# Two blocks of layer-norm work moved out of the attended tiles and in between incidence products

## The chip, the cores and the metric

The kernel runs on one core of a Trainium2 chip. The metric is the device time of one execution in microseconds (us). The engines are PE (matrix products and transposes), DVE (vector), ACT (activations and copies out of PSUM), POOL (small elementwise work) and SP (which only issues DMAs here).

## What is computed

Four graph layers follow each other on 2048 nodes with 128 features, each on `relu(layernorm(x))`, each added to `x`. Cut to what matters here:

```
# layer 1: two steps of sparse attention, then a layer norm with gain and bias
for n in range(2):
    A  = top_p_attention(Xa)          # softmax rows cut to the largest that hold 0.9, renormed
    Xf = R @ Xf
    Xa = A @ Xa
    Z  = Z + Xf @ U1[n].T + Xa @ U2[n].T
h = X + Z
x = x + (h - mean(h)) / sqrt(var(h) + 1e-5) * ln_g + ln_b
# layer 2: incidence products
h = relu(layernorm(x))
m = adj.T @ h                         # "incidence products" below: 16 row tiles of adj
...
x = x + 0.5 * c + 0.5 * c @ W.T       # c from adj @ (m / sqrt(edge_degree)), degrees and h
```

Two layer norms stand between the attention and the incidence products: the first closes layer 1, the second opens layer 2.

## The kernel before, in words

The 2048 nodes are 16 tiles of 128 rows, in 4 blocks of 4 tiles. The attention works through 8 groups, 4 blocks in each of 2 steps; DVE cuts the rows of one group (a bound by guesses, then the rows above it) while PE multiplies the attended rows of the group before it. Each engine has its own instruction list, written by hand; order on an engine is the order of the code, and engines wait for each other by counting semaphores only.

**An attended tile** (`attend`, PE L481 transposes and L740 products, ACT L1001 copies) turns 16 pieces of 128 columns, ACT copies them out four at a time, PE multiplies them. Between its first two groups of four, PE also turns and projects the result of the tile before (L481, L705 to L707), which ACT writes to `R` with its row sum (L1185), counting `z_ok`.

**The last period** is group 7 on DVE (block 3 of step 1) while PE attends block 2's four tiles. As soon as step 1's results of a block stand in `R`, the block can be normed "ahead". For block b that is, in order:

- `first_norm` on ACT: the mean and four squares with sums (L1210, L1213), then on POOL `nd` (L448), the power `es` (L450) and the product `ri` (L452), in the order that `LN_ORDER` lists the blocks' two norms;
- `first_scaled` on ACT (L1228), four tiles, counting `ln_y`;
- `rows_turned` on PE, four transposes in two halves (L481), `turned_out` on ACT (L1001 into `ST`);
- `rows_summed` on PE, two halves, each twice three products (L785 to L787): gain, old `x` and bias;
- `summed_out` on ACT (L1243 into `K`), counting `ln_x2`, `second_norm` on ACT and POOL, `second_scaled` on ACT (L1257 into `hr`), counting `h2_act`.

`blocks_ahead(k)`, on PE and on ACT, says what of this follows the attended tile k. Before, block 0 and block 1 are interleaved there in halves; what is left of block 1 follows the fourth tile. Then PE runs `multiplied(t)`, an incidence product of tile t: four 128x512 products (L798) into PSUM banks 0 to 3. Four tiles of it come before block 2's norm, six after. Then PE attends the four tiles of block 3, turns, and finishes the products 10 to 15.

`multiplied(t)` waits for its adjacency tile, a 1 MB load from HBM which SP issues when the product four before has freed its buffer, and for `h2_act` of its block, 4 per block:

```
pe.wait_ge(here, count)
if t < RING:
    pe.wait_ge(h2_act, G * (t // G + 1))
```

On DVE, `under` of tile k in group 7 (L1419) waits for the last transposes of the attended tile k on PE, since it writes over what they read; `masked` (four L1419 at the group's end) follows the search for the cut.

Of the kernel before, what the change touches and what calls it, by code (L numbers as in the profile page):

```python
# [16 lines left out]
NT = N // P  # L17
DA = 64
BK = 512
G = BK // P  # L20
# [74 lines left out]
def gnn_kernel(nc, x, adj, W0, b0, W1, W2, W3, U1, U2, ln_g, ln_b, L2W, L3W, b3, out):  # L95
# [18 lines left out]
    with ExitStack() as ctx:  # L114
# [101 lines left out]
        def bank(b):  # L216
            return PS[:, b, :]
# [49 lines left out]
        LN_ROOTS = 3 * NB + 5  # L267
        AHEAD_BLOCKS = NB - 1
        RING = G * AHEAD_BLOCKS
        LN_ORDER = ((0, 0), (1, 0), (0, 1), (1, 1), (2, 0), (2, 1))  # L270
        ORDER = (1, 2, 3, 0)

        def natural(t):
# [4 lines left out]
            return (nat_in[t % G], 16 * (NB + 1 + t // G)) if t < RING else (nat_eb[t % G], 16)  # L278

        def turned_at(b, h):  # L280
            return bank(h if b < 2 else 4 + h)

        def summed_at(b, h):
            return bank(2 + h if b < 2 else 6 + h)

        def normed_at(b, second):

# [189 lines left out]
        def _(pe):  # L477
# [8 lines left out]
            with pe.Fori(0, NB) as i:  # L486
                for s in range(G):
                    t = i * G + s
# [274 lines left out]
            def rows_turned(b, h):  # L763

                pe.wait_ge(ln_y, G * (b + 1))
                if b == 1:
                    pe.wait_ge(ln_ts, h + 1)
                for k in range(2):
                    tr = turn(turned_at(b, h)[:, k * P:(k + 1) * P], R[:, G * b + 2 * h + k, :])
                tr.then_inc(ln_t, 1)  # L770

            def rows_summed(b, h):

                pe.wait_ge(ln_ts, 2 * b + h + 1)
                if b == 0:
                    pe.wait_ge(late_in, 16)
                    pe.wait_ge(bc_dma, 3 * 16)
                    pe.wait_ge(diag_ok, 1)
                elif b == 1:
                    pe.wait_ge(ln_x2, 2 * (h + 1))  # L780
                else:
                    pe.wait_ge(z_ok, NT + RING)
                for k in range(2):
                    to = summed_at(b, h)[:, k * P:(k + 1) * P]
                    pe.matmul(to, ST[0][:, (2 * h + k) * P:(2 * h + k + 1) * P], WT[:, U1T, :], start=True, stop=False)  # L785
                    pe.matmul(to, ident[:, :], K[:, G * b + 2 * h + k, :], start=False, stop=False)
                    mm = pe.matmul(to, ident[:, :], BC[:, LNB, :], start=False, stop=True)  # L787
                mm.then_inc(ln_x, 1)

            def multiplied(t):  # L790
                here, count = natural_in(t)
# [3 lines that stand above are left out]
                else:  # L795
                    pe.wait_ge(h2_ok, 1)
                for n in range(4):
                    mm = pe.matmul(bank(n), hr[:, t, :], natural(t)[:, n * BK:(n + 1) * BK],  # L798
                                   start=(t == 0), stop=(t == NT - 1))
                mm.then_inc(m_mm, 1)  # L800

            def blocks_ahead(k):

                if k > 0:
                    rows_summed((k - 1) // 2, (k - 1) % 2)
                rows_turned(k // 2, k % 2)

            def later_keys(n):

# [4 lines left out]
            for step in range(STEPS):  # L814
# [61 lines left out]
                if step == 0:  # L876
# [5 lines left out]
                    for k in range(G):  # L882
                        attend(0, NB - 1, k)

            rows_summed(1, 1)
            pe.wait_ge(ln_x2, 2 * G)
            for t in range(G):
                multiplied(t)
            for h in range(2):
                rows_turned(2, h)  # L890
                rows_summed(2, h)
            for t in range(G, 2 * G + 2):
                multiplied(t)
            for k in range(G):
                attend(1, NB - 1, k)
# [58 lines left out]
            for i in range(NB):  # L954
                b = ORDER[i]
# [38 lines left out]
        def _(act):  # L994
# [14 lines left out]
            for i in range(NB):  # L1009
                for s in range(G):  # L1010
                    t = i * G + s
# [204 lines left out]
            def first_norm(b):  # L1216

                act.wait_ge(z_ok, NT + G * (b + 1))
                if b > 0:
                    act.wait_ge(ln_sq, G * (normed_at(b, 0) - 1))  # L1220
                squared_rows(b, R)

            def first_scaled(b):

                act.wait_ge(ln_root, normed_at(b, 0))
                for k in range(G):
                    t = b * G + k
                    act.activation(R[:, t, :], R[:, t, :], ACT.Identity, scale=es[:, t:t + 1], bias=ri[:, t:t + 1])\  # L1228
                       .then_inc(ln_y, 1)

            def turned_out(b, h):

                act.wait_ge(ln_t, 2 * b + h + 1)
                if b > 0:
                    act.wait_ge(ln_x, 2 * (b - 1) + h + 1)
                copy(ST[0][:, 2 * h * P:2 * (h + 1) * P], turned_at(b, h)[:, 0:2 * P]).then_inc(ln_ts, 1)

            def summed_out(b, h):

                act.wait_ge(ln_x, 2 * b + h + 1)  # L1240
                for k in range(2):
                    t = b * G + 2 * h + k
                    act.activation(K[:, t, :], summed_at(b, h)[:, k * P:(k + 1) * P], ACT.Copy,  # L1243
                                   accum_out=rs[:, t:t + 1]).then_inc(ln_x2, 1)
# [15 lines left out]
            def blocks_ahead(k):  # L1260

                if k == 0:
                    first_scaled(0)
                    turned_out(0, 0)
                    first_norm(1)
                elif k == 1:
                    summed_out(0, 0)
                    turned_out(0, 1)
                    first_scaled(1)
                elif k == 2:  # L1270
                    summed_out(0, 1)
                    turned_out(1, 0)
                    second_norm(0)
                else:
                    summed_out(1, 0)
                    turned_out(1, 1)
                    second_scaled(0)

            for step in range(STEPS):
                if step == 1:  # L1280
                    keys_of(1, 3)
                for k in range(G):
                    exponential(step, 0, k)
                guess(step, 0)
                queries(step, 1)
                u = sum(UNITS_IN[:NB * step])
                for g in range(NB):
                    last = sum(UNITS_IN[:NB * step + g + 1])
                    more = g < NB - 1

                    def unit_next():
                        nonlocal u
                        if u < last:
                            unit(u)
                            u += 1

                    if more:
                        exponential(step, g + 1, 0)
                    elif step == 0:
                        keys_of(1, 0)  # L1300
                        keys_of(1, 1)
                        queries(1, 0)
                    if step == 1 and not more:
                        act.wait_ge(un_z, 2 * UNITS)
                        first_norm(0)
                    for k in range(G):
                        if g > 0:
                            attend(step, g - 1, k, (lambda: guess(step, g + 1)) if more and k == G - 1 else None)
                            if step == 1 and not more:
                                blocks_ahead(k)  # L1310
                        if g == 0 and k > 0:
                            exponential(step, 1, k)
                        if g > 0 and more and k < G - 1:
                            exponential(step, g + 1, k + 1)
                        if g == 0:
                            if k == G - 1:
                                guess(step, 1)
                            unit_next()
                    if g < NB - 2:
                        queries(step, g + 2)  # L1320
                    if more:
                        sums_below(step, g + 1, 0, (0, 1, 2, 3))
                        unit_next()
                        sums_below(step, g + 1, 1, (0, 1))
                        unit_next()
                        sums_below(step, g + 1, 1, (2,))
                    while u < last:
                        unit_next()
                if step == 0:
                    keys_of(1, 2)  # L1330
                else:
                    summed_out(1, 1)
                    second_norm(1)
                    first_norm(2)
                    second_scaled(1)
                    first_scaled(2)
                    for h in range(2):
                        turned_out(2, h)
                        summed_out(2, h)
                    second_norm(2)  # L1340
                    second_scaled(2)
                for k in range(G):
                    attend(step, NB - 1, k)
# [11 lines left out]
            for i in range(NB + 1):  # L1355
                if i > 0:
                    c = i - 1
                    b = ORDER[c]
# [922 lines left out]
```

## Time and profile before

| | us |
|---|---|
| median of 3 runs | 1136.21 (1132.78 to 1137.52) |
| the profiled execution | 1135.15, its span 1133.4 |
| PE busy | 839.8 (74%) |
| DVE busy | 766.4 (68%) |
| ACT busy | 508.6 (45%) |
| POOL busy | 69.2 (6%) |
| mean granted clock of PE | 0.883 of full |

The span is cut into stretches with different limits. In a row in order of time the first number is the start in us from the span's beginning, the second the length; [idle before <-releaser] says how long the engine had stood still and what ended it. PE's clock is granted at either of two levels, 1.0 (2.4 GHz) or 0.5 (1.2 GHz) in the windows.

### The profile page before, as it was taken

The page shows a single profiled execution, that of the slowest core. Times are in us where ns is not written, and L with a number is a line of the kernel's source. Part 1 is how long each engine was busy: PE and PEld are TensorE (multiplying, and loading weights), DVE is VectorE, ACT ScalarE, POOL GpSimd, SP SyncE. Part 2 cuts the span into 40 slices and gives each one's busy share as a digit, 9 for nine tenths or more (in the row PEclk, how much of TensorE's full clock was granted, in tenths as well). Part 3 has the DMA queues.
Part 4 walks back from the last instruction along what each step waited for, and adds up shares of the span by engine and source line. Part 5 has one row for each costly group of instructions (what it writes and reads, how often), then busy time and mean ns, then how long its engine had stood idle before and what let it go on. Part 6 is the DMA issues. An engine that isn't in the chain of part 4 may idle for free.

```text
span 1133.4 us, 12143 instructions
## 1 busy us (share of the span) xinstructions
PE 839.8 (74%) x3886; PEld 566.2 (50%) x3886; DVE 766.4 (68%) x2271; ACT 508.6 (45%) x972; POOL 69.2 (6%) x65
## 2 busy tenths in 40 slices
PE   5789968844786768659778177678568999995496
PEld 5744325622655656555455055557466484552142
DVE  5968689879959969932897797798686302323533
ACT  4876231365476486224213835935946241123011
POOL 0120110000000000000000000000031000003111
PEclk9889979876998989979788589989879999997698
DMA  9869013210022022000134000400340657300000
GB/s 343 308 237 413 19 74 129 99 70 2 1 75 75 1 74 75 1 1 1 40 109 148 1 1 1 149 1 1 112 156 24 252 245 297 149 1 1 1 10 28
DMA packets 18731, 105.48 MB, mean 93 GB/s; under 512 B 1744, under 2 KB 7392, under 8 KB 8416
## 3 DMA queue, kind: packets, MB, share of 16 engines
q1 hardware_dynamic: 17264, 104.02, 24.7%
q10 hardware_dynamic: 1392, 0.61, 0.2%
q8 instruction: 29, 0.48, 0.2%
q14 instruction: 46, 0.38, 0.1%
HBM read 85.74 MB, written 18.88 MB: 92 GB/s over the span
## 4 chain that ended last, share of the span: by engine, by line
PE 37%; DVE 29%; issue 15%; ACT 14%; POOL 2%; DMA 1%; DVEq 1%; POOLq 0%; SPq 0%; ACTq 0%
DVE AT L1419 12%; PE PS L740 8%; PE PS L611 5%; PE PS L985 5%; ACT BC L1168 5%; PE PS L678 5%; ACT AT L1168 4%; DVE mxv L1557 4%; PE PS L481 4%; PE PS L798 3%; DVE nd L1422 3%; PE PS L547 2%; DVE se L1412 1%; DVE AT L1977 1%; ACT AT L1001 1%
## 5 line engine op out<-in xcount | busy, mean ns | idle before, releaser
L678 PE MATMUL PS<-K,ST 128*128 128x512 f32 x224 | 127.3, 721 | 90.7 <-ACT EA L1136 66.3
L1001 ACT ACTIVATE AT<-PS 128x512 f32<-128x512 f32 (+2 forms) x240 | 118.5, 558 | 131.9 <-PE PS L481 117.8
L678 PEld LDWEIGHTS PS<-K,ST 128*128 128x128 f32 x224 | 49.7, 234 | 153.3 <-issue 153.2
L481 PE MATMUL PS<-ident,AT 128*128 128x128 f32 x544 | 82.5, 285 | 49.1 <-DVE rS L2017 24.2
L1419 DVE SCALAR_TENSOR_TENSOR AT<-EA,se 128x2048 uint8<-128x2048 f32 (+1 forms) x50 | 116.8, 2345 | 1.1 <-PE PS L481 0.2
L481 PEld LDWEIGHTS PS<-ident,AT 128*128 128x128 f32 x544 | 66.2, 147 | 57.8 <-ACT AT L1001 26.2
L1419 DVE SCALAR_TENSOR_TENSOR AT<-AT 128x2048 uint8<-128x2048 f32 (+2 forms) x44 | 86.7, 1971 | 11.1 <-PE PS L481 10.2
L1557 DVE TENSOR_REDUCE mxv<-PS 128x1 f32<-128x2048 f32 x32 | 73.1, 2285 | 23.5 <-PE PS L678 18.0
L1977 DVE MAX8 AT<-AT 128x8 f32<-128x256 f32 x256 | 88.4, 412 | 0.8
L1001 ACT ACTIVATE ST<-PS 128x512 f32<-128x512 f32 (+3 forms) x43 | 24.0, 560 | 127.7 <-PE PS L985 36.2
L740 PE MATMUL PS<-AT 128*128 128x128 f32 x512 | 70.1, 287 | 13.0 <-ACT AT L1001 12.6
L740 PEld LDWEIGHTS PS<-AT 128*128 128x128 f32 x512 | 65.0, 199 | 18.1 <-ACT AT L1001 16.2
L985 PE MATMUL PS<-AT,XT 128*128 128x512 f32 x128 | 57.1, 605 | 21.5 <-DVEq L2224 21.5
L740 PE MATMUL PS<-hr,AT 128*128 128x128 f32 x512 | 68.3, 282 | 5.6 <-ACT AT L1001 4.8
L740 PEld LDWEIGHTS PS<-hr,AT 128*128 128x128 f32 x512 | 63.3, 194 | 10.4 <-ACT AT L1001 8.5
L1136 ACT ACTIVATE AT<-PS,negmax 128x2048 f32<-128x2048 f32 x16 | 31.5, 1966 | 81.1 <-DVE negmax L1416 79.9
L547 PE MATMUL PS<-AT,hr 128*128 128x256 f32 x256 | 60.1, 389 | 2.2 <-DVE gs L1416 1.2
L611 PE MATMUL PS<-AT,R 128*128 128x512 f32 x128 | 59.5, 619 | 1.2 <-ACT WT L1001 1.2
L547 PE MATMUL PS<-AT 128*128 128x256 f32 x256 | 58.7, 382 | 1.6 <-DVE gs L1416 1.1
L1168 ACT ACTIVATE AT<-AT 128x2048 uint8<-128x2048 f32 x28 | 55.8, 1993 | 6.9 <-DVEq L2000 6.9
L961 PE MATMUL PS<-AT,R 128*128 128x512 f32 x128 | 57.3, 592 | 0.0
L1168 ACT ACTIVATE BC<-AT 128x2048 uint8<-128x2048 f32 x28 | 55.7, 1990 | 0.0
(287 smaller groups left out, 1423.2 us busy)
## 6 DMA issues: line engine op xcount, KB each, us to landing
AT<-keep_at SPq DMA_DIRECT2D x32, 1024.0 KB, 5.1
EA<-in_adj SPq DMA_DIRECT2D x28, 1024.0 KB, 6.5
keep_at<-AT SPq DMA_DIRECT2D x8, 2048.0 KB, 24.9
AT<-keep_at SPq DMA_DIRECT2D x7, 2048.0 KB, 12.9
AT<-in_adj SPq DMA_DIRECT2D x4, 1024.0 KB, 10.0
EA<-keep_degrees SPq DMA_DIRECT2D x1, 1024.0 KB, 6.4
keep_x<-K SPq DMA_DIRECT2D x4, 256.0 KB, 6.8
out<-EA SPq DMA_DIRECT2D x4, 256.0 KB, 2.3
```

What stands on the lines that cost most here:

```text
L481: return pe.transpose(dst, src, ident[0:p, 0:p])
L547: mm = pe.matmul(bank(6)[:, 2 * P:4 * P], left[:, j, :], slab[:, j, :], start=(j == 0), stop=(j == NT - 1))
L611: mm = pe.matmul(halves(4 + b % 2), R[:, j, :], AT[:, 2 * b:2 * b + 2, j, :], start=(j == 0), stop=(j == NT - 1))
L678: mm = pe.matmul(bank(half(gi, k) + n), ST[1][:, k * P:(k + 1) * P], wide_keys[:, n * BK:(n + 1) * BK], start=True, stop=True)
L740: mm = pe.matmul(bank(6)[:, 0:P], stg[b % 2][:, n * P:(n + 1) * P], left[:, j, :], start=(j == 0), stop=(j == NT - 1))
L961: mm = pe.matmul(halves(4 + i % 2), R[:, j, :], AT[:, 2 * b:2 * b + 2, j, :], start=(j == 0), stop=(j == NT - 1))
L985: mm = pe.matmul(halves(4 + b % 2), XR[:, j, :], AT[:, 2 * b:2 * b + 2, j, :], start=(j == 0), stop=(j == NT - 1))
L1001: return act.activation(dst, src, ACT.Copy)
L1168: act.activation(act_junk[f], E[:, k, :], func, scale=-1.0, bias=th[:, k:k + 1], accum_out=below[:, f, k:k + 1]).then_inc(sum_ok, 1)
L1419: return dve.scalar_tensor_tensor(out=o, in0=x0, scalar=s, in1=x1, op0=op0, op1=op1, **k)
L1557: v(dve.tensor_reduce(mxv[:, odd:odd + 1], PS[:, b:b + 4, :], AX.XY, ALU.max))
L1977: v.put(dve.max(tops[0][:, k, s * TOP:(s + 1) * TOP], cands[k][:, s * N // SETS:(s + 1) * N // SETS]))
```

## The change

- `blocks_ahead` norms block 0 alone inside the attended tiles: all its transposes after tile 1, all its sums after tile 2. On ACT, `first_scaled(0)` follows tile 0, both `turned_out` tile 1, both `summed_out` and `second_norm` tile 2, `second_scaled` tile 3.
- Block 1 is normed wholly after the fourth tile, block 2 after it, between the incidence products: transposes of block 1 after product 1, its sums after product 2, transposes of block 2 after product 3, its sums after product 4. Products 5 to 9 follow.
- Block 1's halves use PSUM banks 4 to 7, as block 2's. `LN_ORDER`, by which POOL works, follows.

```
-        LN_ORDER = ((0, 0), (1, 0), (0, 1), (1, 1), (2, 0), (2, 1))
+        LN_ORDER = ((0, 0), (0, 1), (1, 0), (1, 1), (2, 0), (2, 1))
...
-            return bank(h if b < 2 else 4 + h)
+            return bank(h if b == 0 else 4 + h)
...
# PE, blocks_ahead
-                if k > 0:
-                    rows_summed((k - 1) // 2, (k - 1) % 2)
-                rows_turned(k // 2, k % 2)
+                for h in range(2):
+                    if k == 1:
+                        rows_turned(0, h)
+                    elif k == 2:
+                        rows_summed(0, h)
...
# PE, after the attended tiles
-            rows_summed(1, 1)
-            pe.wait_ge(ln_x2, 2 * G)
-            for t in range(G):
-                multiplied(t)
-            for h in range(2):
-                rows_turned(2, h)
-                rows_summed(2, h)
-            for t in range(G, 2 * G + 2):
+            multiplied(0)
+            multiplied(1)
+            both(rows_turned, 1)
+            multiplied(2)
+            both(rows_summed, 1)
+            multiplied(3)
+            both(rows_turned, 2)
+            multiplied(4)
+            both(rows_summed, 2)
+            for t in range(5, 2 * G + 2):
                 multiplied(t)
...
# ACT, blocks_ahead
                 if k == 0:
                     first_scaled(0)
+                elif k == 1:
                     turned_out(0, 0)
-                    first_norm(1)
-                elif k == 1:
+                    turned_out(0, 1)
+                elif k == 2:
                     summed_out(0, 0)
-                    turned_out(0, 1)
-                    first_scaled(1)
-                elif k == 2:
                     summed_out(0, 1)
-                    turned_out(1, 0)
                     second_norm(0)
                 else:
-                    summed_out(1, 0)
-                    turned_out(1, 1)
                     second_scaled(0)
...
# ACT, after the attended tiles
+                    first_norm(1)
+                    first_scaled(1)
+                    turned_out(1, 0)
+                    turned_out(1, 1)
+                    summed_out(1, 0)
                     summed_out(1, 1)
                     second_norm(1)
                     first_norm(2)
                     second_scaled(1)
                     first_scaled(2)
-                    for h in range(2):
-                        turned_out(2, h)
-                        summed_out(2, h)
+                    turned_out(2, 0)
+                    turned_out(2, 1)
+                    summed_out(2, 0)
+                    summed_out(2, 1)
                     second_norm(2)
                     second_scaled(2)
```

PE after the attended tiles, in the kernel before (L798 is a product, four to a tile; L481 on `R` a block's transposes; L785 to L787 the sums, here of block 2):

```order
L798 MATMUL PS<-EA,hr 128x512 x16
L481 MATMUL PS<-ident,R 128x128 x2
L785 MATMUL PS<-WT,ST 128x128
...
L798 MATMUL PS<-EA,hr 128x512 x24
```

And now, the sums again cut to their first row:

```order
L798 MATMUL PS<-EA,hr 128x512 x8
L481 MATMUL PS<-ident,R 128x128 x4
L798 MATMUL PS<-EA,hr 128x512 x4
L785 MATMUL PS<-WT,ST 128x128
...
L798 MATMUL PS<-EA,hr 128x512 x4
L481 MATMUL PS<-ident,R 128x128 x4
L798 MATMUL PS<-EA,hr 128x512 x4
...
L798 MATMUL PS<-EA,hr 128x512 x20
```

Where four products in a row led to block 2's transposes, one product now stands between block 1's sums and them.

ACT at the same place, before (from the last attended tile's result: block 1's first half, block 0's second norm scaled, block 1's second half; L1210 and L1213 are a norm's mean and squares, of `K` the second, of `R` the first):

```order
L1185 ACTIVATE R,rs<-PS 128x128
L1243 ACTIVATE K,rs<-PS 128x128 x2
L1001 ACTIVATE ST<-PS 128x256
L1257 ACTIVATE hr<-K,ri,es 128x128 x4
L1243 ACTIVATE K,rs<-PS 128x128 x2
L1210 ACTIVATE Dn<-rs 128x4
L1213 ACTIVATE ST,nd<-K,Dn 128x128 x4
L1210 ACTIVATE Dn<-rs 128x4
L1213 ACTIVATE ST,nd<-R,Dn 128x128 x4
L1257 ACTIVATE hr<-K,ri,es 128x128 x4
L1228 ACTIVATE R<-R,ri,es 128x128 x4
```

And now, with line numbers that are 9 higher (L1266 is L1257 of before, and so on), as far as block 1's sums:

```order
L1194 ACTIVATE R,rs<-PS 128x128
L1266 ACTIVATE hr<-K,ri,es 128x128 x4
L1219 ACTIVATE Dn<-rs 128x4
L1222 ACTIVATE ST,nd<-R,Dn 128x128 x4
L1237 ACTIVATE R<-R,ri,es 128x128 x4
L1010 ACTIVATE ST<-PS 128x256 x2
L1252 ACTIVATE K,rs<-PS 128x128 x4
L1219 ACTIVATE Dn<-rs 128x4
L1222 ACTIVATE ST,nd<-K,Dn 128x128 x4
```

Block 0's last scaling now follows the last attended result directly, and block 1's first norm stands behind it, not ahead of it.

## Rows read from the trace of the kernel before

**Rows 1.** Busy time by engine in the stretch 870 to 911 us.
```profile
870.00:911.00 41.00, 39.04 (x118) 19.14 (x117) 17.27 (x60) 13.60 (x55) 4.25 (x9) 1.00 0.64 234
```

**Rows 2.** PE in order of time: start, us, line, operation, count, [idle before <-releaser].
```profile
837.37 2.07 PE L740 MATMUL PS<-AT 128*128 128x128 f32 x8 [1.40 <-ACT AT L1001]
...
844.83 0.39 PE L785 MATMUL PS<-WT,ST 128*128 128x128 f32 x2
...
849.33 1.16 PE L740 MATMUL PS<-AT 128*128 128x128 f32 x8 [1.79 <-ACT AT L1001]
...
854.60 0.39 PE L785 MATMUL PS<-WT,ST 128*128 128x128 f32 x2
...
859.35 1.16 PE L740 MATMUL PS<-AT 128*128 128x128 f32 x8 [2.04 <-ACT AT L1001]
...
866.49 0.39 PE L707 MATMUL PS<-XT,ident 128*128 128x128 f32 x2
...
871.53 14.00 PE L798 MATMUL PS<-EA,hr 128*128 128x512 f32 x32 [0.71 <-ACT K L1243]
...
885.37 0.38 PE L481 MATMUL PS<-ident,R 128*128 128x128 f32 x2
...
886.22 0.49 PE L785 MATMUL PS<-WT,ST 128*128 128x128 f32 x2 [0.47 <-ACT ST L1001]
...
888.81 0.49 PE L785 MATMUL PS<-WT,ST 128*128 128x128 f32 x2 [0.77 <-ACT ST L1001]
...
890.25 20.77 PE L798 MATMUL PS<-EA,hr 128*128 128x512 f32 x48
...
910.86 1.04 PE L481 MATMUL PS<-ident,AT 128*128 128x128 f32 x8
```

**Rows 3.** ACT in order of time, same columns.
```profile
832.44 1.65 ACT L1228 ACTIVATE R<-R,ri,es 128x128 f32<-128x128 f32 x4 [1.56 <-POOL ri L452]
...
836.74 1.22 ACT L1001 ACTIVATE AT<-PS 128x512 f32<-128x512 f32 x3
...
869.03 1.64 ACT L1257 ACTIVATE hr<-K,ri,es 128x128 f32<-128x128 f32 x4
...
871.50 0.20 ACT L1210 ACTIVATE Dn<-rs 128x4 f32<-128x4 f32 x1
...
873.48 0.20 ACT L1210 ACTIVATE Dn<-rs 128x4 f32<-128x4 f32 x1
...
877.13 1.65 ACT L1228 ACTIVATE R<-R,ri,es 128x128 f32<-128x128 f32 x4 [0.22 <-POOL ri L452]
```

**Rows 4.** POOL in order of time, same columns.
```profile
827.88 2.98 POOL L450 TENSOR_TENSOR es<-nd,ex 128x4 f32<-128x4 f32 x1
...
830.94 1.46 POOL L452 TENSOR_TENSOR ri<-Dn,es 128x4 f32<-128x4 f32 x1
...
874.96 0.20 POOL L452 TENSOR_TENSOR ri<-Dn,es 128x4 f32<-128x4 f32 x1
```

**Rows 5.** DVE in order of time, same columns.
```profile
830.01 2.34 DVE L1419 SCALAR_TENSOR_TENSOR AT<-AT 128x2048 uint8<-128x2048 f32 x1
...
862.98 2.35 DVE L1419 SCALAR_TENSOR_TENSOR AT<-AT 128x2048 f32<-128x2048 f32 x1 [4.92 <-PE PS L481]
...
879.60 2.35 DVE L1419 SCALAR_TENSOR_TENSOR AT<-AT,s 128x2048 f32<-128x2048 f32 x1 [2.00 <-issue]
...
889.01 0.18 DVE L2017 RECIPROCAL rS<-Sk 128x4 f32<-128x4 f32 x1
```

**Rows 6.** PE by stretch: length, busy (instructions), granted clock, DMA share, GB/s.
```profile
830.50:834.20 3.70, 0.00 (x0) 1.00 1.01 427
835.50:841.50 6.00, 4.60 (x22) 0.50 0.00 1
842.00:844.00 2.00, 2.00 (x20) 1.00 0.00 0
```

**Rows 7.** DMA issues of the page: count, size, median us from issue to landing.
```profile
EA<-in_adj SPq DMA_DIRECT2D x28, 1024.0 KB, 6.5
```

More of the change, by code:

```diff
@@ L280, in turned_at @@
         def turned_at(b, h):
-            return bank(h if b < 2 else 4 + h)
+            return bank(h if b == 0 else 4 + h)
         def summed_at(b, h):
-            return bank(2 + h if b < 2 else 6 + h)
+            return bank(2 + h if b == 0 else 6 + h)
         def normed_at(b, second):
@@ L765, in rows_turned @@
                 pe.wait_ge(ln_y, G * (b + 1))
-                if b == 1:
-                    pe.wait_ge(ln_ts, h + 1)
+                if b == 2:
+                    pe.wait_ge(ln_ts, 2 + h + 1)
                 for k in range(2):
@@ L779, in rows_summed @@
                 elif b == 1:
-                    pe.wait_ge(ln_x2, 2 * (h + 1))
+                    pe.wait_ge(z_ok, NT + RING)
                 else:
-                    pe.wait_ge(z_ok, NT + RING)
+                    pe.wait_ge(ln_x2, G + 2 * (h + 1))
                 for k in range(2):
@@ L883, in _, with both @@
                         attend(0, NB - 1, k)
-            rows_summed(1, 1)
-            pe.wait_ge(ln_x2, 2 * G)
-            for t in range(G):
-                multiplied(t)
-            for h in range(2):
-                rows_turned(2, h)
-                rows_summed(2, h)
-            for t in range(G, 2 * G + 2):
+            def both(part, b):
+                for h in range(2):
+                    part(b, h)
+            multiplied(0)
[8 more added lines that the diff above has]
+            for t in range(5, 2 * G + 2):
                 multiplied(t)
```

## The prediction

> **What bounds the kernel here.** I first read the busy time by stretch. From 870 to 911 us PE is busy for 39.04 of 41.00 us at the full clock, DVE for 17.27 and ACT for 13.60 [rows 1]. Then the instructions in order of time on each engine. PE's first incidence product begins at 871.53, ended by ACT's last `K` row; PE reaches block 3's attended tiles at 910.86 without an idle time in its row, though DVE had what they need (`rS`, L2017) at 889.01 [rows 2, 5]. So DVE has 22 us to spare, and PE's own queue decides when the rest of the kernel starts. Everything behind 910.86 hangs on block 3 and keeps its order; its DMAs start from PE's or ACT's progress. I take it to move as a whole, so the question is how far that one point moves.
>
> **1. The attended tiles: PE gets ahead.** In each step I keep the shown durations and take out what the change takes out.
>
> Tile 1: its first products waited for ACT's copies, which began at 836.74, because ACT still did block 1's first norm behind `first_scaled(0)`. That one ends at 832.44 + 1.65 = 834.09 [rows 3], and now the copies follow it: 2.65 us earlier. Products begin at 837.37 - 2.65 = 834.72, and the tile, which ended at 844.83 [rows 2], ends at 842.2 if the low clock ends earlier too.
>
> Between tile 1 and tile 2's products lay 849.33 - 844.83 = 4.50 us [rows 2]: a half of sums, a half of transposes and ACT's work on both, with block 1's four scalings. Now four transposes (0.85), then tile 2's own eight transposes beside two short copies out on ACT (an estimate of 0.4 each, a third of the 1.22 us for three at 836.74 [rows 3]) and the 0.63 us that a copy takes until the products start (836.74 to 837.37). Estimate 2.1 us, products at 844.3; the body of a tile is 854.60 - 849.33 = 5.27 us [rows 2], so it ends at 849.6.
>
> Between tile 2 and tile 3: both halves of sums. One block's transposes and sums took 890.25 - 885.37 = 4.88 us, of which 0.47 and 0.77 were waits that the rows show [rows 2]. Less those, and some 0.1 to start again behind them, 3.55 us of work, which I split by its instructions into 0.85 of transposes and 2.7 of sums. 849.6 + 2.7 = 852.3. ACT then copies the last half out (0.8 from the last sum), does `second_norm(0)` (1.8; block 1's took from 871.50 to before the next norm's mean at 873.48 [rows 3]) and copies for tile 3: products at 852.3 + 0.8 + 1.8 + 0.63 = 855.5 instead of 859.35.
>
> Tile 3 and its result: 866.49 + 0.39 - 859.35 = 7.53 us [rows 2], to 863.0. ACT writes `R` (0.4) and then scales block 0 at once (1.64, as at 869.03 [rows 3]). Product 0 starts at **865.1 instead of 871.53: 6.4 us earlier**. In the attended tiles no DVE wait stands in the way: `under` waited for PE, 4.92 us at 862.98 [rows 5], and moves ahead by 3.9 us with it.
>
> **2. Block 1 comes back, between products.** A product is 13.84 / 4 = 3.46 us (871.53 to 885.37), later 20.61 / 6 = 3.44 [rows 2]. Products 0 and 1 last until 872.0. Beside them ACT and POOL do `first_norm(1)` (2.0 and 1.8) and `first_scaled(1)` (1.65): 865.1 + 5.4 = 870.5, hidden with 1.5 us to spare; if that cover were gone, 1.5 us of delay is free and the rest counts. Transposes to 872.9, product 2 to 876.3, sums to 879.0, product 3 to **882.5**. Cost of block 1's work on PE: 3.55 us, of no use to anything else. The copies of its transposes (0.8) lie beside product 2. The banks 4 to 7 are free, PE having had its last attended result copied.
>
> **3. The new wait.** Block 2's transposes need `first_scaled(2)`. On ACT that stands behind block 1's outputs, its second norm and its second scaling. Before, this chain ran from 871.50 to 877.13 + 1.65 = 878.78, 7.3 us [rows 3], beside four products (13.8 us), and cost PE nothing. Now it starts when block 1's last sum is copied out, 879.0 + 0.8 = 879.8, and only one product, to 882.5, covers it. With the durations of before it ends at 887.1: PE waits 4.6 us. Queued behind the waiting transposes are all further products, block 3's attended tiles and so the rest. Product 4 would have to wait anyhow, for block 1's `h2_act`, 1.9 us less long.
>
> POOL makes it longer. POOL's product `ri` takes 0.20 us at 874.96, but 1.46 us at 830.94, ending at 832.40, just behind a DVE operation of two full tiles which ends at 830.01 + 2.34 = 832.35; the power at 827.88 took 2.98 us beside the same kind [rows 4, 5]. DVE's `masked` is four such operations from 879.60 [rows 5], which now start 3.9 us earlier, 875.7, and run to 884.8. Block 1's second norm asks POOL at 882: I let `ri` wait for the last of them, until 885.0. Then ACT scales (1.65) and `first_scaled(2)`, whose roots are in by then, ends at 888.3. PE resumes at **888.5, after 6.0 us of idling**. Bounds: no hold-up gives 887.3, two full ones as around 830 (3.2 us together) give 890.6. I take the middle since one of the four is still running.
>
> The Trainium skill (SBUF — State Buffer, "Who interferes with whom") says that a DVE instruction with two SBUF inputs contends with a GpSimd instruction that reads SBUF, the later one waiting. The trace agrees, by the 1.46 us against 0.20; were the page wrong and the long POOL rows due to something else, the sum would be 1.2 us smaller.
>
> **4. The rest at full clock.** 888.5 + 0.85 transposes = 889.4; product 4 to 892.8; sums to 895.5 (before, block 2 cost 4.88 with its waits, so 1.3 us come back here); products 5 to 9, 17.2 us, to **912.7. That is 1.8 us later** than 910.86. Sum: -6.4 + 3.55 + 6.0 - 1.3 = +1.85. Block 2's second norm (needed by product 8) is ready near 902, before product 8's start at 905.8.
>
> **5. The clock.** After PE had stood still for 3.70 us at 830.5 the granted clock was 0.50 from 835.5 to 841.5, though PE worked again from 834.2; it was full from 842 [rows 6]. From the products at 837.37 to 842 are 4.6 us at the lower level [rows 2, 6]. The new idle time of 6.0 us is longer than that one, so I take the clock to fall in it and to come back 4.6 us after PE resumes: half of that, **2.3 us**, is lost. Bounds: nothing, if it does not fall, and 3.5 us, if it stays down for 7, which is about 835 to 842.
>
> The Trainium skill (TensorE: Matmul & The Clock Gate, "HAM oscillation") states that an idle gap in which PE waits re-throttles it and that the work behind it starts cold. By that the sum is +4.1, and without it +1.8; the row agrees.
>
> **6. DMA.** Tile 4's load is issued when product 0 is done, now 868.6 instead of 875, and lands in some 6.5 us [rows 7]; product 4 starts at 889. Later loads have at least three products, 10 us. Nothing.
>
> **Sum.** +1.8 + 2.3 = +4.1 us. The profiled execution took 1135.15 us for a span of 1133.4, so it would be 1139.3; it lies 1.06 under the median, 1136.21, against which I give **1140.3**, 0.36% more. A measurement of this kernel can tell about 0.5%, 5.7 us, from no change.
>
> **The rivals.**
> - **The wait is short and the clock holds.** POOL is not held (-1.2) and no clock is lost: +0.6, 1136.8. For it: the hold-up depends on which of four DVE operations is running. Against it: the wait is then still 4.6 us, longer than the 3.70 that was followed by the low clock.
> - **Slower.** The wait at block 2's transposes decides: both POOL operations are held (+2.1 over mine) and the clock stays low for 7 us (+1.2): +7.4, 1143.6. It is beyond 0.5% from the point where the wait passes 7.6 us with 2.3 us lost to the clock, or 6.4 us with 3.5. For it: the slow pair at 827.88 and 830.94. Against it: by then DVE has one or two of those operations left.
> - **A little faster.** PE idles less in tile 1, since its transposes no longer wait for `first_scaled(0)`. If the clock came back at 838.5, 3.3 us of low clock less, 1.6 us are gained; with a short wait and a held clock, +0.6 - 1.6 = -1.0, 1135.2. Even with no wait at all and no clock lost, the sum is 1.8 - 6.0 = -4.2, so over 0.5% faster needs something that I don't see.
>
> **Chances.** Forecast 0.50; short wait 0.20; slower 0.22; a little faster 0.08. Over 0.5% faster 0.03 (what I overlooked), within 0.5% 0.70, slower 0.27 (the slower case, and the forecast's upper edge). The range takes in -1.0 and +7.4 and some spread of the median: 1135.0 to 1144.0.
>
> **What would show it.** In the profile after: product 0 near 865; PE's idle time before block 2's four transposes near 6 us, put down to ACT's `R` scalings (L1237 there); the POOL `ri` before block 1's second scaling over 1 us; granted clock 0.50 in the first products behind it, so that product 4 takes over 5 us where 3.44 is normal; block 3's attended tiles at 915 instead of 910.86, and everything from there to the end shifted by the same. I am wrong if that wait is under 3 us, if PE idles elsewhere (before block 1's transposes, at product 8), or if the stretch behind 911 changes its own length by more than 1 us.

## The result, and the profile after

Over 18 runs of each kernel the changed one takes 1141.74 us (1139.06 to 1145.04) against 1137.29 us; the ratio of the runs is 1.0046, with a 95% interval of 1.0034 to 1.0057. It is slower, by 0.46%, inside what was called no change (0.5%). The profiled execution:

```profile
span 1139.7 us, 12143 instructions
```

Its span is 6.3 us longer than before's (1133.4). PE's first attended transposes of the last period start 1.01 us later than before (820.07 against 819.06), ahead of anything that the change moves; I call that the 1.0 us from upstream. From there to block 3's attended tiles it is 917.19 - 820.07 = 97.12 us against 910.86 - 819.06 = 91.80: **5.3 us more**. From there to the span's end it is 222.5 us in both. The rest behind block 3's start moved as a whole.

PE in order of time, changed kernel, where before stood [rows 2] (start, length, line, shapes, count, [idle before <-releaser]):

```profile
866.24 10.05 PE L798 MATMUL PS<-EA,hr 128*128 128x512 f32 x16 [2.08 <-ACT hr L1266]
...
876.13 0.60 PE L481 MATMUL PS<-ident,R 128*128 128x128 f32 x4
...
880.00 0.38 PE L785 MATMUL PS<-WT,ST 128*128 128x128 f32 x2
...
882.68 3.60 PE L798 MATMUL PS<-EA,hr 128*128 128x512 f32 x8
...
890.85 1.12 PE L481 MATMUL PS<-ident,R 128*128 128x128 f32 x4 [4.58 <-ACT R L1237]
...
891.76 5.74 PE L798 MATMUL PS<-EA,hr 128*128 128x512 f32 x8
...
897.34 0.38 PE L785 MATMUL PS<-WT,ST 128*128 128x128 f32 x2
...
900.02 17.33 PE L798 MATMUL PS<-EA,hr 128*128 128x512 f32 x40
...
917.19 1.04 PE L481 MATMUL PS<-ident,AT 128*128 128x128 f32 x8
```

Product 0 is at 866.24; less the 1.0 us from upstream that is 865.2, where 865.1 was forecast. Then read the lengths. Products 0 and 1 take 9.89 us (866.24 to 876.13), not 6.9. PE waits 4.58 us for ACT's scaling of block 2. Transposes, product 4 and sums take 9.17 us (890.85 to 900.02), where the same work at full clock takes 6.6 (893.05 to 899.66 in the run filled, below). Products 5 to 9 are as always, 17.2.

The clock says why. PE of the changed kernel by stretch (length, busy, granted clock, DMA share, GB/s):

```profile
862.00:864.00 2.00, 1.17 (x8) 1.00 0.00 0
864.00:866.00 2.00, 0.16 (x2) 0.84 0.00 0
866.00:868.00 2.00, 1.76 (x2) 0.50 0.01 4
...
870.00:872.00 2.00, 2.00 (x3) 0.50 0.00 0
872.00:874.00 2.00, 2.00 (x6) 0.96 0.24 33
...
888.00:890.00 2.00, 0.00 (x0) 0.81 0.92 385
890.00:892.00 2.00, 1.15 (x5) 0.50 0.16 66
892.00:894.00 2.00, 2.00 (x3) 0.50 0.00 0
...
896.00:898.00 2.00, 2.00 (x10) 0.98 0.00 0
```

and of the kernel before, ahead of its product 0:

```profile
864.00:866.00 2.00, 1.18 (x10) 1.00 0.00 0
866.00:868.00 2.00, 2.00 (x18) 1.00 0.00 0
868.00:870.00 2.00, 1.23 (x11) 1.00 0.01 4
870.00:872.00 2.00, 1.28 (x9) 1.00 0.00 0
```

In the changed kernel the clock falls twice. The second fall, in the wait, was forecast. The first was not: it comes just ahead of product 0, where PE was busy for 1.17 + 0.16 us of 4, and lasts until about 872. In the kernel before, the same place held block 1's sums and transposes between its short waits, and the clock stayed up.

POOL, DVE and ACT of the changed kernel around the new wait:

```profile
885.58 0.51 POOL L448 TENSOR_SCALAR nd<-nd 128x4 f32<-128x4 f32 x1 [15.87 <-ACT ST L1222]
...
886.17 1.01 POOL L450 TENSOR_TENSOR es<-nd,ex 128x4 f32<-128x4 f32 x1
...
883.69 2.34 DVE L1429 SCALAR_TENSOR_TENSOR AT<-AT,s 128x2048 f32<-128x2048 f32 x1
...
887.49 1.65 ACT L1266 ACTIVATE hr<-K,ri,es 128x128 f32<-128x128 f32 x4
...
889.15 1.65 ACT L1237 ACTIVATE R<-R,ri,es 128x128 f32<-128x128 f32 x4
```

DVE's last operation of two full tiles ends at 886.03. POOL's mean row (L448) is 0.51 us long instead of 0.19 and ends right behind it; the power (L450) is 1.01 us, not held. The forecast had POOL held for 1.2 us there. The chain came 3 us later than forecast, by the slow products 0 and 1, and so mostly missed DVE's operations, by which the wait was 4.6 us and not 6.0. The product `ri` (L452), on which the forecast put the 1.2 us, is 0.20 us long.

### The profile page after: what moved, and what is told of

Its sections match the earlier page's. It is cut to its first block, busy times and chain, and to the rows that moved or that the text cites. A ratio compares the mean times of both kernels' runs of the same rounds, so it can differ in the third digit from the quotient of the medians.

```text
span 1139.7 us, 12143 instructions
## 1 busy us (share of the span) xinstructions
PE 844.8 (74%) x3886; PEld 568.7 (50%) x3886; DVE 766.2 (67%) x2271; ACT 509.2 (45%) x972; POOL 68.1 (6%) x65
## 4 chain that ended last, share of the span: by engine, by line
PE 37%; DVE 29%; issue 15%; ACT 14%; POOL 2%; DMA 1%; DVEq 1%; POOLq 0%; SPq 0%; ACTq 0%
DVE AT L1429 12%; PE PS L740 8%; PE PS L611 5%; PE PS L994 5%; ACT BC L1177 5%; PE PS L678 5%; ACT AT L1177 4%; DVE mxv L1567 4%; PE PS L481 4%; PE PS L798 3%; DVE nd L1432 3%; PE PS L547 2%; DVE se L1422 1%; DVE AT L1987 1%; ACT AT L1010 1%
## 5 line engine op out<-in xcount | busy, mean ns | idle before, releaser
L481 PE MATMUL PS<-ident,AT 128*128 128x128 f32 x544 | 81.3, 282 | 49.0 <-DVE rS L2027 24.2
L481 PEld LDWEIGHTS PS<-ident,AT 128*128 128x128 f32 x544 | 65.3, 146 | 57.6 <-ACT AT L1010 26.2
L994 PE MATMUL PS<-AT,XT 128*128 128x512 f32 x128 | 57.1, 605 | 21.5 <-DVEq L2234 21.5
```

Source lines behind the costliest of these rows:

```text
L481: return pe.transpose(dst, src, ident[0:p, 0:p])
L994: mm = pe.matmul(halves(4 + b % 2), XR[:, j, :], AT[:, 2 * b:2 * b + 2, j, :], start=(j == 0), stop=(j == NT - 1))
```

## Experiments

All are edits of the changed kernel unless it says otherwise. Each was timed against the kernel before on its own chip, so across groups I compare ratios to it, and in the traces the time from the first attended transposes of the last period to product 0, from product 0 to block 3's attended tiles, and from there to the span's end (rest). The timed ratios have intervals of some 0.1% to either side, and differences of under 2 us between two of them are left to the traces.

| kernel | ratio to before (95%) | to product 0, us | product 0 to block 3, us | both | rest, us |
|---|---|---|---|---|---|
| before | 1 | 52.5 | 39.3 | 91.8 | 222.5 |
| changed | 1.0046 (1.0034 to 1.0057) | 46.2 | 51.0 | 97.1 | 222.5 |
| filled | 1.0034 (1.0022 to 1.0046) | 46.3 | 48.5 | 94.8 | 223.9 |
| early2 | 1.0031 (1.0020 to 1.0041) | 46.2 | 48.1 | 94.3 | 223.9 |
| pairs | 1.0041 (1.0027 to 1.0054) | 46.2 | 50.8 | 97.0 | 222.6 |
| best | 0.9982 (0.9970 to 0.9994) | 46.2 | 44.1 | 90.3 | 222.5 |
| fill0 | 1.0040 (1.0027 to 1.0054) | 46.2 | 50.8 | 97.0 | 222.6 |
| best_fill0 | 0.9998 (0.9986 to 1.0010) | 46.4 | 45.2 | 91.5 | 223.8 |
| best_fill01 | 0.9985 (0.9969 to 1.0002) | 45.1 | 45.2 | 90.2 | 222.6 |
| fill0_late | 1.0041 (1.0026 to 1.0056) | 46.3 | 47.8 | 94.1 | 224.1 |
| best_fill0_late | 0.9983 (0.9972 to 0.9994) | 46.2 | 41.2 | 87.4 | 224.0 |
| best_fill01_late | 0.9948 (0.9931 to 0.9964) | 43.4 | 41.2 | 84.6 | 223.8 |

No edit touches what lies in the last column, yet it has two values, some 1.3 us apart. PE stands still there for 21.5 us in every trace, and the low clock behind that lasts longer in some: from 155 to 160 us behind block 3's start the mean granted clock is 0.85 or 0.86 in the six traces with the short rest, and 0.54 to 0.61 in the others (probe, below, among them). Why is open. So an edit's worth is read from the column "both", called the stretch below, and a timed ratio is to be set against both and rest together.

### filled: keep the clock up in the wait

```
+            def filled(n):
+                for _ in range(n):
+                    pe.matmul(bank(4), ident[:, :], XT[:, 0:BK], start=True, stop=True)
...
             multiplied(3)
+            filled(5)
             both(rows_turned, 2)
```

> The changed kernel with five 128x512 products of no use (4.3 us of PE at the full clock) ahead of block 2's transposes, where PE stood idle for 4.58 us; nothing reads them. Theory (the wait itself and the clock that falls in it are two costs): the transposes start as before them, the clock stays at 1.00, product 4 takes 3.5 us instead of 5.6, and the time is 2.2 us under the changed kernel, near 1139.5. Rival (the low clock has another cause, or costs nothing in the end): product 4 still takes 5.6 us and the time is that of the changed kernel, 1141.7, or above it if the fillers overrun the wait.

```profile
888.31 4.46 PE L890 MATMUL PS<-XT,ident 128*128 128x512 f32 x10
...
893.05 0.66 PE L481 MATMUL PS<-ident,R 128*128 128x128 f32 x4 [0.29 <-ACT R L1243]
...
893.55 3.60 PE L798 MATMUL PS<-EA,hr 128*128 128x512 f32 x8
```

The fillers (a row of ten, two passes to a product) fit the wait, 0.29 us of it is left, and product 4 takes 3.4 us (893.55 to 896.98, where the sums begin). From product 0 to block 3 it is 2.5 us less than in the changed kernel, and the stretch is 2.3 us shorter. So the wait and the clock are two costs, and the clock's is about the 2.3 us of the forecast. In the timed runs the gain is 0.0012 of 1137, 1.4 us, with overlapping intervals: that this is shown rests on the trace.

### early2 and best: take the chain apart

```
-        LN_ORDER = ((0, 0), (0, 1), (1, 0), (1, 1), (2, 0), (2, 1))
+        LN_ORDER = ((0, 0), (0, 1), (1, 0), (2, 0), (1, 1), (2, 1))
...
# ACT
                     first_norm(1)
+                    first_norm(2)
                     first_scaled(1)
+                    first_scaled(2)
                     turned_out(1, 0)
...
                     second_norm(1)
-                    first_norm(2)
                     second_scaled(1)
-                    first_scaled(2)
```

> The changed kernel with block 2's first norm and first scaling moved ahead on ACT and POOL, right behind block 1's; PE's order unchanged. Theory (the chain from block 1's last sum over both norms to block 2's scaled rows is what PE waits for): PE no longer waits at block 2's transposes, but some 2 us at product 4, for block 1's second scaling; 2.5 us less of waiting, and 2.2 us more if the clock then holds: 1137.0 (1139.2 if it falls all the same). Rival (block 1's work on PE, out of its cover, is the loss, and the wait is merely where it shows): no more than 1 us, 1141.

```profile
887.69 0.60 PE L481 MATMUL PS<-ident,R 128*128 128x128 f32 x4
...
890.86 5.35 PE L798 MATMUL PS<-EA,hr 128*128 128x512 f32 x8 [2.56 <-ACT hr L1266]
```

PE goes from product 3 into block 2's transposes without a wait, and waits 2.56 us at product 4 for block 1's second scaling. The wait at the transposes was the chain over both norms, as the forecast had it; block 2's first norm needs nothing of block 1. The clock still fell (product 4: 5.2 us). The stretch is 2.9 us shorter, between the two values expected; by the ratios it is 1.7 us, with overlapping intervals.

`best` adds two moves:

```
# PE
             both(rows_turned, 2)
-            multiplied(4)
             both(rows_summed, 2)
+            multiplied(4)
...
# ACT
                     second_norm(1)
-                    second_scaled(1)
                     turned_out(2, 0)
                     turned_out(2, 1)
+                    second_scaled(1)
```

> As early2, and block 2's sums ahead of product 4 on PE, with the copies of its transposes ahead of block 1's second scaling on ACT. Theory: no wait over 1 us between product 0 and product 9; 4 to 4.3 us of waiting and 2.2 us of clock less than the changed kernel: 1135.3, under the kernel before by 2 us (0.2%). Rival (PE's clock falls at product 0 anyway, and takes the gain back): 1137 to 1138, the same as the kernel before.

```profile
866.96 10.05 PE L798 MATMUL PS<-EA,hr 128*128 128x512 f32 x16 [2.08 <-ACT hr L1266]
...
887.68 0.49 PE L785 MATMUL PS<-WT,ST 128*128 128x128 f32 x2 [0.25 <-ACT ST L1010]
...
890.47 20.77 PE L798 MATMUL PS<-EA,hr 128*128 128x512 f32 x48
```

No wait over 0.25 us is left between product 0 and block 3, and products 4 to 9 take 20.6 us at full clock. The stretch is 6.8 us shorter than in the changed kernel and the ratio is 0.9982: faster than the kernel before by 0.18%, 2 us. Products 0 and 1 (10.05 us) are still at the low clock; the rival was right that this remains, but not that it takes all the gain.

### pairs: two products as cover instead of one

```
-            multiplied(2)
             both(rows_summed, 1)
+            multiplied(2)
             multiplied(3)
```

> The changed kernel with block 1's sums ahead of product 2 instead of behind it, so that two products (6.9 us) stand between them and block 2's transposes; ACT's and POOL's order unchanged. Theory (one product is too short a cover for a chain of 8.1 us from the last sum): PE waits some 0.8 us for the copies of block 1's transposes and 1.2 us at block 2's, instead of 4.6: 2.6 us less, and 2.2 us of clock: 1136.9. Rival (POOL held by DVE's operations of two full tiles makes the chain longer where it now falls earlier, beside them): the wait is 3 us or more, 1139 or above.

```profile
883.51 7.03 PE L798 MATMUL PS<-EA,hr 128*128 128x512 f32 x16
...
894.33 1.11 PE L481 MATMUL PS<-ident,R 128*128 128x128 f32 x4 [3.78 <-ACT R L1237]
...
886.42 1.16 POOL L448 TENSOR_SCALAR nd<-nd 128x4 f32<-128x4 f32 x1 [12.96 <-ACT ST L1222]
...
887.66 3.00 POOL L450 TENSOR_TENSOR es<-nd,ex 128x4 f32<-128x4 f32 x1
...
885.18 2.35 DVE L1429 SCALAR_TENSOR_TENSOR AT<-AT,s 128x2048 f32<-128x2048 f32 x1
...
887.45 2.35 DVE L1429 SCALAR_TENSOR_TENSOR AT<-AT,s 128x2048 f32<-128x2048 f32 x1
```

The wait is 3.78 us, not 1.2. **Here my theory fell and the rival stands**: the chain now starts earlier, beside DVE's last two operations (885.18 and 887.45), and POOL's mean row takes 1.16 us and its power 3.00, 3 us more than alone. Twice the cover gained only 0.8 us of wait. Block 1's transposes and sums, with a wait of 0.26 us between them, took 0.5 us of it back (879.88 to 883.51, 3.6 us instead of 3.1), and the stretch is as long as in the changed kernel.

### fill0: the clock at product 0, and what it hid

```
# filled(n) as above, into bank 0
+            filled(2)
             multiplied(0)
```

> The changed kernel with two 128x512 products of no use (1.7 us) in PE's wait of 2.08 us ahead of product 0; nothing reads them. Theory (the clock falls at product 0 for want of work in front of it, which the moved block 1 did before; and that loss hid another, DVE holding POOL up): products 0 and 1 take 6.9 us instead of 9.9, but block 1's second norm then asks POOL 3 us earlier beside the last of DVE's four operations, so the wait at block 2's transposes is 6 to 7 us instead of 4.6: 1 to 2 us under the changed kernel, 1140.2. Rival (POOL's long rows are not DVE's doing): the wait stays 4.6 us and the time is 3 us lower, 1138.7. Second rival (the low clock at product 0 has nothing to do with idling): no change.

```profile
865.76 7.10 PE L798 MATMUL PS<-EA,hr 128*128 128x512 f32 x16 [0.36 <-ACT hr L1272]
...
890.10 1.11 PE L481 MATMUL PS<-ident,R 128*128 128x128 f32 x4 [7.25 <-ACT R L1243]
...
882.16 1.19 POOL L448 TENSOR_SCALAR nd<-nd 128x4 f32<-128x4 f32 x1 [12.92 <-ACT ST L1228]
...
883.43 3.00 POOL L450 TENSOR_TENSOR es<-nd,ex 128x4 f32<-128x4 f32 x1
...
880.95 2.35 DVE L1435 SCALAR_TENSOR_TENSOR AT<-AT,s 128x2048 f32<-128x2048 f32 x1
...
883.22 2.35 DVE L1435 SCALAR_TENSOR_TENSOR AT<-AT,s 128x2048 f32<-128x2048 f32 x1
```

Both parts of the theory came. Products 0 and 1 take 6.9 us (865.76 to 872.70): with the idle time ahead of product 0 filled to 0.36 us the clock stays at 1.00. And block 1's second norm, 3 us earlier, meets DVE's operations: 1.19 and 3.00 us on POOL, and PE waits 7.25 us at block 2's transposes. The 3.0 us gained are given back, 2.7 of them in that wait. The stretch is 97.0 us, as in the changed kernel, and the timed ratio 1.0040.

The Trainium skill (SBUF — State Buffer, "Who interferes with whom") has this rule, that a DVE instruction with two SBUF inputs contends with a GpSimd instruction that reads SBUF. The rows of pairs and fill0 agree (1.16 and 1.19 us against 0.19, 3.00 against 1.01), and the next runs do too.

### probe: the hold-up by itself

On the kernel before, at POOL behind block 2's first norm:

```
+                if i == 4:
+                    for m in range(10):
+                        pool.tensor_tensor(probe[:, :], ex[:, 1, 0:G], ex[:, 1, 0:G], ALU.pow).then_inc(probed, 1)
+                        pool.wait_ge(probed, m + 1)
```

> The kernel before with ten more powers of 4 columns on POOL behind block 2's first norm, from about 877 us, each waiting for the one before, into a buffer that nothing reads. DVE's four operations of two full tiles run from 879.6 to 888.7. Theory (such an operation holds POOL back until it ends): a power takes 1.01 us with no such operation beside it, and those issued beside one last up to about 3 us, ending some 1 us behind an end of DVE's. Rival (no hold-up): all ten take 1.01 us and end by 889. The time is that of the kernel before unless block 2's second norm is held up, at most 2 us more.

The ten powers by their line (count, duration in ns min/median/max, first and last start):

```profile
L457 POOL TENSOR_TENSOR probe<-ex x10: 1007/1007/2373, 881.4 to 896.1; 128x4 f32<-128x4 f32 x10
```

Six take 1.01 us, and four, beside DVE, 2.2 to 2.4. They occupy 15.7 us where ten alone would take about 10.8 (an estimate, 1.08 us from one start to the next). While DVE ran its four operations (883.8 to 893.0 here) powers started at 884.65, 887.10, 889.38 and 891.65, some 2.3 us apart, which is DVE's own period of 2.27, and each ended 0.86 us behind an end of DVE's. One POOL instruction gets through per DVE operation. DVE's operations stay at 2.35 us, the first of them too, which started at 883.81 beside a power that had run since 883.57: in these rows only POOL is held. The expected lengths, up to about 3 us, were a little too high; the rival (no hold-up) is out. The one timed run took 1140.63 us against a median of 1139.51 us before, inside the 2 us that were expected at most.

### The same with DVE moved out of the way

```
# DVE, ahead of the last group's four operations
                 load_more()
+                if gi == 2 * NB - 1:
+                    dve.wait_ge(ln_root, 5)
                 masked(v, E)
```

> The run fill0 with one wait more on DVE: in the last group its four operations of two full tiles start only when POOL has done block 1's second and block 2's first norm (their products ri). DVE has some 20 us to spare there. Theory (DVE's operations hold POOL, and that is the difference between the waits of 7.25 us in fill0 and 4.58 us in the changed kernel): POOL's mean row takes 0.2 us and its power 1.01 us, the wait at block 2's transposes is 4.3 to 4.6 us, and with block 0's products at full clock the time is 2.7 us under fill0, 1140.6. Rival (POOL was late for another reason): the wait stays near 7.2 us and the time that of fill0, or above it because DVE now ends late.

```profile
887.60 1.12 PE L481 MATMUL PS<-ident,R 128*128 128x128 f32 x4 [4.58 <-ACT R L1243]
...
882.32 0.19 POOL L448 TENSOR_SCALAR nd<-nd 128x4 f32<-128x4 f32 x1 [12.93 <-ACT ST L1228]
...
882.60 1.01 POOL L450 TENSOR_TENSOR es<-nd,ex 128x4 f32<-128x4 f32 x1
...
885.89 2.35 DVE L1435 SCALAR_TENSOR_TENSOR AT<-AT,s 128x2048 f32<-128x2048 f32 x1 [11.32 <-POOL ri L452]
```

POOL's rows are back at 0.19 and 1.01 us, and the wait is 4.58 us instead of 7.25, by nothing but DVE's start. DVE ends at 895.3 and nobody waits for it. In the trace the stretch is 2.8 us shorter than in fill0, but the rest is 1.5 us longer, by the low clock described under the table. The timed ratio, 1.0041 from five runs against 1.0040, shows no gain; its interval spans 3.4 us. So the cause of the longer wait is shown, and a gain in time is not. All three kernels with the wait on DVE have the long rest in their traces; so have filled, early2, best_fill0 and probe without it, and whether DVE's wait has a part in that is open.

> The run best with two fillers ahead of product 0. Theory: products 0 and 1 take 6.9 us instead of 9.9; the wait for block 1's second scaling at product 4, absent in best, comes back with 1 to 2 us because POOL is held: 1135.3, 1 to 2 us under best. Rival: no hold-up, 3 us under best.

```profile
888.30 22.54 PE L798 MATMUL PS<-EA,hr 128*128 128x512 f32 x48 [2.06 <-ACT hr L1272]
```

`best_fill0` (best with the fillers of fill0) came out above best, not 1 to 2 us under it: 2.06 us of wait came back at product 4, with POOL's rows at 1.21 and 3.00 us, and a low clock with it; 45.2 us from product 0, 1 us more than best. Its ratio is 0.9998 against best's 0.9982, with overlapping intervals.

> best_fill0 with the same wait on DVE. Theory: the wait of 2.06 us at product 4 goes, and with it the low clock behind it (1.7 us in the ten products): 3.5 us under best_fill0, 1135.0, and 2 us under best. Rival (late cuts on DVE delay block 3's attended tiles, or POOL was late otherwise): at or above best_fill0, 1138.6.

```profile
886.52 20.77 PE L798 MATMUL PS<-EA,hr 128*128 128x512 f32 x48
```

With DVE's wait both go: 41.2 us from product 0, 3 us less than best. DVE's operations now hold POOL in block 2's second norm instead (1.47 and 3.00 us), which costs PE nothing: ACT has it scaled by 895.9, and product 8 starts at about 900.3. Its ratio, 0.9983, is 0.0015 under best_fill0, 1.7 us where 4 are gone from the trace, and level with best's within the intervals: of the 2.9 us by which its stretch is shorter than best's, the longer rest takes back 1.5 in the traces. The time alone does not tell them apart.

```
# attended tile 1 of block 2, where PE waits for block 0's scaling
+                            ... else (lambda: filled(4)) if step == 1 and not more and k == 1 else None)
```

> As best_fill0, and four fillers (3.5 us) in the second attended tile of block 2, between the result's transpose and the first products, where PE waits 3.9 us for block 0's scaling on ACT. Theory: the clock, which falls there from about 835 to 842 in every trace so far, stays at 1.00, and tile 1 takes 5.3 us instead of 8.0: 2.7 us under best_fill0, 1132.6. Rival (the wait moves to the next tile, on DVE or ACT): under 1 us.

```profile
857.91 1.16 PE L740 MATMUL PS<-AT 128*128 128x128 f32 x8 [2.13 <-ACT AT L1016]
...
860.00:861.00 1.00, 1.00 (x6) 0.50 0.00 0
```

The trace had 45.1 us to product 0 instead of best_fill0's 46.4: 1.3 us less, not 2.7, because the clock then fell in tile 3 (from 859 to 863). By the ratios it is 1.5 us, with overlapping intervals. Tile 3's products stand behind a wait of 2.13 us in all eleven kernels with the change; the clock fell behind it in this one alone.

> best_fill01 with the same wait on DVE. Theory: as above, 3.5 us under best_fill01, 1133.7, some 0.5% under the kernel before. The fillers in tile 1 kept the clock up there, but it fell in tile 3 instead (859 to 863); if that happens again, 1 to 2 us of this is lost in some executions. Rival: at or above best_fill01, 1137.2.

```profile
834.51 1.16 PE L740 MATMUL PS<-AT 128*128 128x128 f32 x8 [0.22 <-ACT AT L1016]
...
862.36 7.11 PE L798 MATMUL PS<-EA,hr 128*128 128x512 f32 x16 [0.36 <-ACT hr L1272]
...
882.93 20.77 PE L798 MATMUL PS<-EA,hr 128*128 128x512 f32 x48
```

Here the clock stayed up from 827 on. Tile 1's products begin after 0.22 us of idling, product 0 is 43.4 us from the first transposes, and products 4 to 9 take 20.6. **The ratio is 0.9948, interval 0.9931 to 0.9964: 0.5% faster than the kernel before, and by the two ratios 1% faster than the changed one.** That is 5.9 us; in the traces the stretch is 7.2 us shorter than before's and the rest 1.2 longer, so the two agree. Of the kernels run it is the best.

## Why the prediction was right, and where not

1140.3 was forecast against a median of 1136.21, 0.36% more; 0.46% came, within the range. By its steps:

- **What bounds.** Right. The point at which block 3's attended tiles start moved by 5.3 us net of upstream, and in this trace what follows kept its length.
- **Step 1, product 0 6.4 us earlier.** 6.3 us (52.5 to 46.2). But the step priced only when product 0 starts. It left 2.1 us of idling ahead of product 0, behind two short waits, and put nothing for the clock after such a patch. **This is the step that failed**, with step 5, which looked for one long idle time only: 3.0 us in products 0 and 1. Fill0 shows it.
- **Step 2, block 1 between products.** Right, and priced a little too high: transposes and sums take 0.43 + 2.68 = 3.1 us, not 3.55; no wait at its transposes.
- **Step 3, the wait of 6.0 us.** Place, releaser and chain were right (early2 takes it away); its size was 4.6, which is the forecast's own wait without a hold-up. The term for POOL, 1.2 us, was 0.3 here, and it fell on the mean row, not on `ri` (0.20 us), so the sign that the forecast named for it did not show. As a mechanism it was right, and larger than put: 2.7 us once the chain starts where the forecast had it (fill0 against fill0_late), since both the mean row and the power are held.
- **Step 4.** Block 2 without waits: right. What comes back is 4.88 - 3.1 = 1.8 us, not 1.3, as the work was priced too high here too.
- **Step 5, the clock in the wait, 2.3 us.** 2.6 us by lengths (9.17 against 6.6), 2.5 by filled, from product 0 to block 3. The clock fell, as forecast; it stayed down for some 5 us behind PE's start, not 4.6.
- **Step 6, DMA.** Right; no wait for a tile of adjacency anywhere in the stretch.

Forecast -6.4 + 8.2 + 2.3 = +4.1; measured -6.3 + 3.0 (clock at product 0) + 3.1 (block 1) + 4.7 (wait; 4.58 in the row, and what product 3's end adds) - 1.8 (block 2 without its waits) + 2.6 (clock), +5.3. Two errors of opposite sign, +3.0 and -1.3, hang together: had the clock held at product 0, the wait would have been 7.25 us, as fill0 shows with the same total. That the forecast came within 1.2 us is partly owed to that, and so partly luck: single terms were off by up to 3.0 us. Of the rivals, the slower one named the right mechanism (POOL held on both instructions) and it is what happens in pairs and fill0, though the pair held is mean row and power, not power and `ri`. The first half of the short-wait rival did occur: POOL was hardly held and the wait was the 4.6 us that it names. Its second half, that the clock holds, did not. The faster case did not occur.

## What to carry to other kernels

When work is taken out from between short waits, look at what the engine's clock does in the thinned place, not only at when the next product starts. When work is set between products as cover, write down the whole chain that ends in the next use, over all engines, and start first what depends on nothing new: moving block 2's first norm and its sums ahead was worth 6.8 us where twice the cover was worth nothing. An engine with slack can still hold up one on the path; here a wait on DVE, which had 20 us to spare, took 2.7 us off PE's wait in the trace.

## What the runs showed of the hardware

- The clock fell behind an idle time of 2.08 us when two waits of 0.46 and 0.37 us came just before it, in all five traces with that patch unfilled, and in none of the six with two fillers in it. The length of one wait does not settle it: behind a wait of 2.13 us ahead of tile 3's products the clock held in ten of the same eleven traces and fell in one, best_fill01. The Trainium skill (TensorE: Matmul & The Clock Gate, "HAM oscillation") warns of long idle gaps between matmuls; the one here, 2.08 us, is shorter than the 3.70 us that I had taken as the sign [rows 6].
- Products that nothing reads, in PE's own wait, keep the clock up: 3.0 us gained at product 0 for 1.7 us of fillers, 2.5 us at block 2's transposes for 4.3.
- POOL's mean row, with one tensor as input and 0.19 us long, is held by DVE's operations of two tiles as the power is (1.16 to 1.47 us where it starts beside one that still has over 1 us to go, 0.46 to 0.53 where DVE's last ends sooner). DVE's operations are no longer for it, 2.35 us in every row.
